# Second MLP product in fp32r: activations and W2 split into high and low parts

## The chip, the cores and the metric

The kernel runs on one core of a Trainium2 chip. The metric is the device time of one execution in microseconds, median of several runs.

## The reference

Layer 0 is a mixture of experts over x of shape (16, 256, 256), 16 units of 256 tokens with 256 features. Layers 1 to 3 are transformer blocks of the same form: modulated layer norm (plain affine in layer 3), self attention with 16 heads of 16, cross attention to 77 context tokens, and an MLP. What the change touches is the MLP of each block, here layer 1's:

```python
x_norm2 = modulate(_ln(x), shift_m, scale_m)
h = jax.nn.gelu(x_norm2 @ W_mlp1 + b_mlp1)
h = h @ W_mlp2 + b_mlp2
x = x + gate_m[:, None] * h
```

W_mlp1 is 256 x 1024, W_mlp2 (called W2 here) 1024 x 256. In layers 2 and 3 the same weights are named fc1_w, fc2_w and ffn_w1, ffn_w2.

## The kernel before, in words

**Two stages.** The function mixture() runs layer 0 for 16 units, one per step. The function blocks() runs layers 1 to 3 as 48 units u (layer u // 16 + 1, input u % 16) in a software pipeline that is written out by hand: every engine (SP, GpSimd, ScalarE, VectorE, TensorE) has its own list of calls, and in the loop over n TensorE does self attention of unit n - 2, cross attention of n - 3, and the MLP of n - 4 and n - 5 in one mixed order. Engines meet through counting semaphores, `S["..."]`. What an engine does next is fixed by its list: a late input holds everything behind it.

**Split products.** Most products of the blocks are done in fp32r with both operands in two parts: high = the value rounded to fp32r, low = value - high. Three products (high by high, low by high, high by low; `TERMS`) are added in PSUM. High parts of activations are made by a cast or copy, low parts by a subtraction. The weights' parts for layers 1 to 3 are made once, in the mixture stage. There a piece of 256 x 256 is loaded into one of two buffers `raw`, ScalarE copies it to the high part (`piece_high`, L920), GpSimd subtracts (`piece_low`, L792), and SP stores both parts to DRAM (`store_piece`, L703). There are 24 pieces, two in each of twelve steps, after the step's other calls. load_piece(k) (L697) waits for piece_low(k - 2), and piece_high(k) also waits for the store of piece k - 2. In blocks() ScalarE's queue loads the parts (`load_split`, L2079) for the next layer once the last unit of a layer has used the old ones.

**The second MLP product** is not split. `up` (L3028, fp32r) makes a quarter of the hidden layer in each of four calls, `up_act` (L1988) applies GELU and writes h_c, and `down(d, j)` (L3183), j from 0 to 7, does two fp32 matmuls each: eight chunks of h_c for the first 128 tokens, then eight for the second. An fp32 matmul shows as two records in the profile. W2 is double buffered between layers, loaded directly with the other weights of `layer_loads`. TensorE does down 0 to 3 in a row and 4 to 7 apart, between the scores of both attentions.

**Around it**, in the same unit of the loop: VectorE takes the row maxima of the self attention's plain scores in eight calls `self_max` (L2477, tile m_a), multiplies the heads by reciprocals (oT_a and oT_b, L2469), and normalises x before cross attention (`cross_normed`, L2439, tile xn_b, not in layer 3); TensorE then turns xn_b (`cross_turned`, L3019) and makes the keys of the next unit from xT_a (L3028), whose two parts VectorE writes (L2519, L2523). GpSimd computes the reciprocal deviations (L1798, L1801), the residual sums (L1790), o_gated (L1848) and the last sum into y_c (L1870). SP copies the head rows q_hl, k_hl, qc_hl into q_cat, k_cat, qc_cat (L1420), 18 DMAs for these three in one unit. In `self_plain` (L3079) TensorE reads q_cat and k_cat.

## Time and profile before

| | us |
|---|---|
| median of 3 runs (2870.46 to 2873.42) | 2873.33 |
| the profiled execution | 2874.42 |
| its span, first to last instruction | 2872.6 |
| TensorE busy (matmuls) | 2745.2, 96% |
| VectorE busy | 1732.0, 60% |
| ScalarE busy | 1548.3, 54% |
| GpSimd busy | 687.1, 24% |

Busy time of an engine is the union of its instructions; matmuls overlap each other, so a length of one matmul is more than its share of a run, and runs are measured from their start to the start of the next instruction. An instruction's row gives its start, its length, and how many alike are merged. The mixture stage fills about the first 650 us, the blocks the rest.

### The profile page before, as it was taken

The page shows a single profiled execution, that of the slowest core. Times are in us where ns is not written, and L with a number is a line of the kernel's source. Part 1 is how long each engine was busy: PE and PEld are TensorE (multiplying, and loading weights), DVE is VectorE, ACT ScalarE, POOL GpSimd, SP SyncE. Part 2 cuts the span into 40 slices and gives each one's busy share as a digit, 9 for nine tenths or more (in the row PEclk, how much of TensorE's full clock was granted, in tenths as well). Part 3 has the DMA queues.
Part 4 walks back from the last instruction along what each step waited for, and adds up shares of the span by engine and source line. Part 5 has one row for each costly group of instructions (what it writes and reads, how often), then busy time and mean ns, then how long its engine had stood idle before and what let it go on. Part 6 is the DMA issues. An engine that isn't in the chain of part 4 may idle for free.

```text
span 2872.6 us, 61852 instructions
## 1 busy us (share of the span) xinstructions
PE 2745.2 (96%) x23508; PEld 2279.8 (79%) x23508; DVE 1732.0 (60%) x3584; ACT 1548.3 (54%) x2703; POOL 687.1 (24%) x759
## 2 busy tenths in 40 slices
PE   7999999995899999999999999999999999999998
PEld 6999999993577777777777777777777777777876
DVE  2444444434676776766766667667566666666642
...
GB/s 162 45 79 80 70 70 70 40 9 132 95 82 116 100 103 122 94 107 124 106 145 97 98 118 93 112 117 93 128 102 136 115 85 112 103 94 105 103 69 38
DMA packets 276950, 277.90 MB, mean 97 GB/s; under 512 B 90352, under 2 KB 206432, under 8 KB 276656
## 3 DMA queue, kind: packets, MB, share of 16 engines
...
## 4 chain that ended last, share of the span: by engine, by line
PE 64%; DVE 7%; issue 3%; ACT 2%; DMA 1%; SPq 0%; POOL 0%; POOLq 0%; DVEq 0%; ACTq 0%
PE gbank L3183 12%; PE obank L3028 10%; PE gbank L3028 7%; PE obank L3035 6%; PE score L3093 4%; PE obank L3113 4%; DVE m_a L2477 4%; PE obank L3159 3%; PE score L3079 3%; PE score L3142 2%; DVE x_a L2439 2%; PE gbank L3128 2%; PE obank L3128 2%; PE gbank L3019 2%; PE gbank L3043 2%
## 5 line engine op out<-in xcount | busy, mean ns | idle before, releaser
L1971 ACT ACTIVATE p_f<-score 128x1024 f32<-128x1024 f32 (+1 forms) x576 | 567.8, 1021 | 293.7 <-PE score L3093 264.6
L2477 DVE TENSOR_REDUCE m_a<-score 128x4 f32<-128x1024 f32 x384 | 459.9, 1219 | 159.0 <-PE score L3079 158.8
L3183 PE MATMUL gbank<-w,h_c 128*128 128x256 f32 x1536 | 387.9, 392 | 1.9 <-ACT h_c L1988 1.9
L3183 PEld LDWEIGHTS gbank<-w,h_c 128*128 128x128 f32 x1536 | 279.2, 191 | 44.9 <-ACT h_c L1988 2.3
L1150 PE MATMUL m_ps<-m_comb,m_w 128*128 128x256 f32 x2304 | 295.4, 284 | 1.5 <-PEq L254 1.5
L1150 PEld LDWEIGHTS m_ps<-m_comb,m_w 128*128 128x128 f32 x2304 | 279.9, 188 | 5.0 <-issue 3.6
L2487 DVE TENSOR_REDUCE m_b<-gbank 128x4 f32<-128x308 f32 x192 | 92.1, 480 | 265.1 <-PE gbank L3128 241.6
L823 ACT ACTIVATE m_hf<-m_ps,tab 128x256 f32<-128x256 f32 x192 | 80.7, 471 | 246.8 <-PE m_ps L1150 246.8
L1848 POOL TENSOR_TENSOR o_gated<-w_o,gate_a 128x512 f32<-128x512 f32 x48 | 62.3, 1298 | 591.0 <-PE obank L3035 591.0
L765 POOL TENSOR_TENSOR m_hhl<-m_hf,m_hhl 128x512 fp32r<-128x512 f32 x96 | 125.3, 1306 | 318.6 <-DVE m_hhl L989 318.6
L3113 PE MATMUL obank<-p_f,v_s 128*20 128x256 f32 x3072 | 199.9, 390 | 0.6 <-ACT p_f L1971 0.4
L3093 PE MATMUL score<-q_cat,k_cat 50*128 50x256 f32 x1536 | 190.2, 318 | 8.4 <-DMA q_cat<-mT_a 6.5
L3093 PEld LDWEIGHTS score<-q_cat,k_cat 50*128 50x128 f32 x1536 | 132.1, 188 | 53.8 <-issue 36.3
L3028 PE MATMUL gbank<-xT_c,w_up 128*128 128x256 f32 x1152 | 170.7, 299 | 2.6 <-DVE xT_c L2519 2.3
L1790 POOL TENSOR_TENSOR res_b<-x_b,b_oc 128x512 f32<-128x512 f32 x48 | 61.2, 1276 | 455.0 <-DVE x_c L2646 455.0
L3028 PE MATMUL obank<-xT_a,w_qkv 128*128 128x256 f32 x1152 | 165.7, 293 | 3.6 <-DVE xT_a L2519 3.2
L989 DVE CAST m_hhl<-m_hf 128x512 fp32r<-128x512 f32 x96 | 41.0, 427 | 212.4 <-ACT m_hf L823 212.4
L3028 PE MATMUL obank<-xT_c,w_up 128*128 128x256 f32 x1152 | 163.3, 292 | 0.1
L3028 PEld LDWEIGHTS gbank<-xT_c,w_up 128*128 128x128 f32 x1152 | 151.2, 196 | 13.1 <-issue 2.7
L3028 PEld LDWEIGHTS obank<-xT_c,w_up 128*128 128x128 f32 x1152 | 145.6, 193 | 19.9 <-issue 19.4
L3079 PE MATMUL score<-k_cat,q_cat 48*128 48x256 f32 x1536 | 155.3, 310 | 5.8 <-DVE m_a L2477 3.6
L3028 PEld LDWEIGHTS obank<-xT_a,w_qkv 128*128 128x128 f32 x1152 | 149.8, 195 | 7.3 <-issue 4.1
...
## 6 DMA issues: line engine op xcount, KB each, us to landing
q_cat<-q_hl SPq DMA_DIRECT2D x288, 128.0 KB, 3.7
k_cat<-k_hl SPq DMA_DIRECT2D x288, 128.0 KB, 4.0
qc_cat<-qc_hl SPq DMA_DIRECT2D x288, 128.0 KB, 3.1
split_L<-m_cut SPq DMA_DIRECT2D x24, 512.0 KB, 5.7
x_a<-x_after_L SPq DMA_DIRECT2D x48, 256.0 KB, 2.7
x_b<-x_after_L SPq DMA_DIRECT2D x48, 256.0 KB, 4.4
kc_cat<-kc_hl SPq DMA_DIRECT2D x288, 39.0 KB, 1.9
x_after_L<-y_c SPq DMA_DIRECT2D x32, 256.0 KB, 2.4
```

What stands on the lines that cost most here:

```text
L765: e.tensor_tensor(h_hl[:, 1, at:at + 2, :], h_f[:, i % 3, :, :], h_hl[:, 0, at:at + 2, :].bitcast(F32), ALU.subtract).then_inc(S["hl"].sem, 1)
L1150: mm = e.matmul(b.ap[:, m, :], w1[:, wp, k, 2 * i + m, :], c[:, cp, k, :], start=(k + wp + cp == 0), stop=(k == 3 and wp == 1))
L1971: e.activation(p_f[i % 4][0:n, :], score[i % 2].ap[0:n, :, :].rearrange("p h n -> p (h n)"), ACT.Exp, scale=SCALE).then_inc(ex.sem, 1)
L2477: e.tensor_reduce(m_a[:, :, i::NPAIR].rearrange("p t h -> p h t"), score[i % 2].ap[:, :, :].rearrange("p h (t k) -> p h t k", t=TT), AX.X, ...
L2487: e.tensor_reduce(m_b[:, :, 8 * hf + 2 * i:8 * hf + 2 * i + 2].rearrange("p t j -> p j t"), B_KP[hf].ap[:, :, :].rearrange("p t (j k) -> p ...
L3028: mm = e.matmul(bank.ap[:, m, :], w[:, wp, i, m * P:(m + 1) * P], xT[:, xp, i, :], start=(wp + xp + i == 0), stop=(xp == 1 and i == CC - 1))
L3035: mm = e.matmul(bank.ap[:, tt, :], xT[:, i, tt * P:(tt + 1) * P], w[:, i, :], start=(i == 0), stop=(i == CC - 1))
L3079: mm = e.matmul(bank.ap[:, hf, tt * NT:(tt + 1) * NT], qm[64 * hf:64 * hf + QROWS, i, tt * P:(tt + 1) * P], km[64 * hf:64 * hf + QROWS, i, ...
L3093: mm = e.matmul(bank.ap[:, hf, kc * NT:(kc + 1) * NT], ka[64 * hf:64 * hf + QROWS + 2, i, kc * P:(kc + 1) * P], qa[64 * hf:64 * hf + QROWS ...
L3113: mm = e.matmul(bank.ap[32 * g:32 * g + VW, i % 2, :], v_s[:, kc, 8 * j + 2 * i + hf, :], pf[:, at:at + NT], start=(kc == 0), stop=(kc == ...
L3128: mm = e.matmul(view[:, j, tt, 0:CPAD], qc_cat[64 * hf:64 * hf + QROWS, 2 * i + j, tt * P:(tt + 1) * P], kc_cat[64 * hf:64 * hf + QROWS, 2 ...
L3183: mm = e.matmul(B_DOWN.ap[:, tt, :], h_c[:, k, tt * P:(tt + 1) * P], weights_of(d)["w2"][:, k, :], start=(k == 0), stop=(k == MC - 1))
```

## The change

`down` becomes a split product: 48 fp32r matmuls a unit in place of 16 fp32 ones. `up_act` writes GELU's result to h_f, two slots of a quarter each. VectorE casts each quarter to h_c's high part (`mlp_h_high`), GpSimd subtracts for the low part (`mlp_h_low`), and `up_act` of quarter i waits for the low part of quarter i - 2. W2 is cut in the mixture stage too: 36 pieces in place of 24, three a step in twelve steps. Its parts are single buffered, 2 MB a layer, loaded by ScalarE's queue after the last unit of a layer has used them (`next_down`).

```diff
         def layer_buffers(stack, i):
             sb = buffers(stack)
             return dict(
-                kvc=sb(f"w_kvc{i}", [P, CC, 2 * D]), w2=sb(f"w_2{i}", [P, MC, D]),
+                kvc=sb(f"w_kvc{i}", [P, CC, 2 * D]),
                 bv=sb(f"b_v{i}", [P, D]), bvc=sb(f"b_vc{i}", [P, D]), boc=sb(f"b_oc{i}", [P, D]))
...
-        split = [None] + [scratch(f"split_L{i}", (8, P, 2 * CC * D)) for i in (1, 2, 3)]
-        W_in = signals(nc, "w", {}, dict(qk=2, v=1, qc=1, up0=2, up1=2, o=1, oc=1))
+        split = [None] + [scratch(f"split_L{i}", (12, P, 2 * CC * D)) for i in (1, 2, 3)]
+        W_in = signals(nc, "w", {}, dict(qk=2, v=1, qc=1, up0=2, up1=2, down=4, o=1, oc=1))
         WT = [None, layer_buffers(root, 1)]
         s_last = nc.alloc_semaphore("last_x_after_L0")
         s_w = [nc.alloc_semaphore(f"weights_L{L}") for L in range(4)]
...
             for i in range(2):
                 loads.append((w["kvc"][:, :, i * D:(i + 1) * D], chunks(kvc[i])))
-            for i in range(0, MC, 2):
-                loads.append((w["w2"][:, i:i + 2, :], chunks(p["w2"][i * P:(i + 2) * P, :])))
             return loads
...
             p = layer_parts(L)
-            return [chunks(w[:, at:at + D]) for w in p["qkv"] + [p["qc"], p["w1"]] for at in range(0, w.shape[1], D)]
-
-        n_w = [0, 9, 9, 9]
+            return ([chunks(w[:, at:at + D]) for w in p["qkv"] + [p["qc"], p["w1"]] for at in range(0, w.shape[1], D)]
+                    + [chunks(p["w2"][at:at + D, :]) for at in range(0, MLP, D)])
+
+        n_w = [0, 5, 5, 5]
...
         N_ITER = NB + 2
+
+        def pieces_of(n):
+            return range(3 * n - 6, 3 * n - 3)
+
...
-                for i in range(2):
-                    store_piece(2 * n - 6 + i)
-                    load_piece(2 * n - 4 + i)
+                for k in pieces_of(n):
+                    store_piece(k - 2)
+                    load_piece(k)
...
-                for i in range(2):
-                    piece_low(2 * n - 4 + i)
+                for k in pieces_of(n):
+                    piece_low(k)
...
-                for i in range(2):
-                    piece_high(2 * n - 4 + i)
+                for k in pieces_of(n):
+                    piece_high(k)
```

In blocks():

```diff
         W = dict(W, qkv=sb("w_qkv", [P, 3, 2, CC, D], F32R), qc=sb("w_qc", [P, 1, 2, CC, D], F32R),
-                 up=sb("w_up", [P, MLP // D, 2, CC, D], F32R))
+                 up=sb("w_up", [P, MLP // D, 2, CC, D], F32R),
+                 down=sb("w_down", [P, MLP // D, 2, CC, D], F32R))
         st_p, st_t, st_k, st_c = stats("p"), stats("t"), stats("k"), stats("c")
         bias_a, gate_a = sb("bias_a", [P, D]), sb("gate_a", [P, D])
...
         bias_c, gate_c = sb("bias_c", [P, D]), sb("gate_c", [P, D])
-        h_c, y_c = sb("h_c", [P, MC, NT]), tile("y_c")
+        h_f, h_c, y_c = sb("h_f", [P, 2, 2, NT]), sb("h_c", [P, 2, MC, NT], F32R), tile("y_c")
 
         score = [Bank(stack.enter_context(nc.psum_tensor(f"score{i}", [P, 2, 512], F32))) for i in range(2)]
...
 
+            def mlp_h_low(c, i):
+                if live(c):
+                    e.wait_ge(*S["C_hh"].at(c, i + 1))
+                    e.tensor_tensor(h_c[:, 1, 2 * i:2 * i + 2, :], h_f[:, i % 2, :, :],
+                                    h_c[:, 0, 2 * i:2 * i + 2, :].bitcast(F32), ALU.subtract).then_inc(S["C_hl"].sem, 1)
+
...
                 e.wait_ge(*S["C_hp"].at(u, i + 1))
-                if u and i == 0:
-                    e.wait_ge(*S["C_down"].at(u - 1))
+                if i >= 2:
+                    e.wait_ge(*S["C_hl"].at(u, i - 1))
+                elif u:
+                    e.wait_ge(*S["C_hl"].at(u - 1, i + 3))
                 for j in range(2):
                     m = 2 * i + j
-                    ac = e.activation(h_c[:, m, :], B_UP[i].ap[:, j, :], gelu,
+                    ac = e.activation(h_f[:, i % 2, j, :], B_UP[i].ap[:, j, :], gelu,
                                       bias=bcols[layer(u)][:, 8 + m:9 + m])
                 ac.then_inc(S["C_h"].sem, 1)
 
...
+            def next_down(d):
+                if last_of_layer(d):
+                    e.wait_ge(*S["C_down"].at(d))
+                    load_split(layer(d) + 1, "down", "down", 8, (0, 1, 2, 3))
+
...
+                load_split(1, "down", "down", 8, (0, 1, 2, 3))
...
                     x_low(c, xn_c[:, :, :], xT_c, S["C_xh"], S["C_xl"])
+
+            def mlp_h_high(c, i):
+                if not live(c):
+                    return
+                e.wait_ge(*S["C_h"].at(c, i + 1))
+                if c and i == 0:
+                    e.wait_ge(*S["C_down"].at(c - 1))
+                e.tensor_copy(h_c[:, 0, 2 * i:2 * i + 2, :], h_f[:, i % 2, :, :]).then_inc(S["C_hh"].sem, 1)
 
             def self_stats(q):
...
             def down(d, j):
                 if not live(d):
                     return
+                tt, i = divmod(j, MC // 2)
                 if j == 0:
-                    e.wait_ge(*S["C_h"].at(d))
+                    weights_in(d, "down")
                     turn(B_DOWN, S["C_y"], d)
-                for i in (2 * j, 2 * j + 1):
-                    tt, k = divmod(i, MC)
-                    mm = e.matmul(B_DOWN.ap[:, tt, :], h_c[:, k, tt * P:(tt + 1) * P], weights_of(d)["w2"][:, k, :],
-                                  start=(k == 0), stop=(k == MC - 1))
+                if tt == 0:
+                    e.wait_ge(*S["C_hh"].at(d, i + 1))
+                for wp, xp in TERMS:
+                    if xp and tt == 0:
+                        e.wait_ge(*S["C_hl"].at(d, i + 1))
+                    for c in range(CC):
+                        mm = e.matmul(B_DOWN.ap[:, tt, :], h_c[:, xp, 2 * i + c, tt * P:(tt + 1) * P],
+                                      W["down"][:, i, wp, c, :], start=(i + wp + xp + c == 0),
+                                      stop=(i == MC // 2 - 1 and xp == 1 and c == CC - 1))
                 if j == MC - 1:
                     mm.then_inc(S["C_down"].sem, 1)
```

The lists of the engines are rotated by some calls in the loop (their bodies start at another place of the same cycle), and the new calls stand in them. Everything else keeps its order on every engine. Where the new calls of VectorE and GpSimd stand, one turn of the loop:

```diff
+                self_max(n - 2, 2)
+                self_max(n - 2, 3)
+                self_max(n - 2, 4)
+                mlp_h_high(n - 5, 0)
+                self_max(n - 2, 5)
+                mlp_h_high(n - 5, 1)
+                self_heads_normed(n - 3)
+                self_max(n - 2, 6)
...
+                cross_stats(n - 3)
+                self_max(n - 2, 7)
+                mlp_h_high(n - 5, 2)
+                cross_normed(n - 3)
+                self_x_high(n - 1)
+                self_x_low(n - 1)
+                self_max_low(n - 2)
+                cross_x_low(n - 3)
                 context_stats(n - 2)
...
+                mlp_h_high(n - 5, 3)
+                cross_heads_normed(n - 4)
```

```diff
+                self_rstd(n - 1)
+                mlp_sum(n - 6)
+                self_residual(n - 3)
+                mlp_h_low(n - 5, 0)
+                mlp_h_low(n - 5, 1)
+                self_out_gated(n - 2)
+                mlp_residual(n - 5)
+                cross_rstd(n - 3)
+                mlp_h_low(n - 5, 2)
+                mlp_h_low(n - 5, 3)
+                cross_residual(n - 3)
```

**VectorE, in a unit of layer 1**, from the statistics of x_b to the parts of xT_b. Before:

```order
L2608 TENSOR_TENSOR vc_s<-obank,b_vc 77x16x16
L2425 BN_STATS t_st<-x_b 128x6 x2
L2430 BN_AGGR t_mv<-t_st 128x2 x2
L2477 TENSOR_REDUCE m_a<-score 128x2x2
L2439 TENSOR_SCALAR xn_b<-x_b,t_mv,t_rstd 128x256 x2
L2519 CAST xT_a<-x_a 128x512
L2523 TENSOR_TENSOR xT_a<-x_a,xT_a 128x512
L2495 TENSOR_TENSOR mT_a<-gbank,mT_a 16x256
L2523 TENSOR_TENSOR xT_b<-gbank,xT_b 128x512
```

Now:

```order
L2735 TENSOR_TENSOR vc_s<-obank,b_vc 77x16x16
L2544 BN_STATS t_st<-x_b 128x6 x2
L2549 BN_AGGR t_mv<-t_st 128x2 x2
L2596 TENSOR_REDUCE m_a<-score 128x2x2
L2670 CAST h_c<-h_f 128x512
L2558 TENSOR_SCALAR xn_b<-x_b,t_mv,t_rstd 128x256 x2
L2638 CAST xT_a<-x_a 128x512
L2642 TENSOR_TENSOR xT_a<-x_a,xT_a 128x512
L2614 TENSOR_TENSOR mT_a<-gbank,mT_a 16x256
L2642 TENSOR_TENSOR xT_b<-gbank,xT_b 128x512
```

A CAST of a quarter of h stands between the last TENSOR_REDUCE of the self scores and xn_b. Two more stand ahead of this place, behind the fifth and the sixth of the eight TENSOR_REDUCE, and one behind xT_b.

**GpSimd, the same unit**, from the sum into x_b to the residual of the next stage. Before:

```order
L1790 TENSOR_TENSOR x_b<-x_b,bias_a 128x512
L1848 TENSOR_TENSOR o_gated<-w_o,gate_a 128x512
L1790 TENSOR_TENSOR res_c<-x_c,bias_c 128x512
L1798 TENSOR_TENSOR t_rstd<-t_mv,eps 128x2
L1801 TENSOR_TENSOR t_rstd<-t_rstd,minus_half 128x2
L1790 TENSOR_TENSOR res_b<-x_b,b_oc 128x512
```

Now:

```order
L1818 TENSOR_TENSOR x_b<-x_b,bias_a 128x512
L1897 TENSOR_TENSOR h_c<-h_f,h_c 128x512 x2
L1876 TENSOR_TENSOR o_gated<-w_o,gate_a 128x512
L1818 TENSOR_TENSOR res_c<-x_c,bias_c 128x512
L1826 TENSOR_TENSOR t_rstd<-t_mv,eps 128x2
L1829 TENSOR_TENSOR t_rstd<-t_rstd,minus_half 128x2
L1897 TENSOR_TENSOR h_c<-h_f,h_c 128x512 x2
L1818 TENSOR_TENSOR res_b<-x_b,b_oc 128x512
```

Two subtractions for h stand ahead of o_gated, and two directly behind t_rstd.

**ScalarE, at the end of a mixture step.** m_cut is the high part of a weight piece, m_hf the next unit's hidden activations. Before:

```order
L904 ACTIVATE m_rex,m_rsm<-m_lg,m_rmx 128x3 x2
L912 ACTIVATE m_gp<-m_gp 128x512
L920 ACTIVATE m_cut<-m_raw 128x512 x2
L823 ACT_TABLE_LOAD
L823 ACTIVATE m_hf<-m_ps,tab 128x256 x2
L843 ACTIVATE m_ctxT<-m_ps 128x154
```

Now:

```order
L907 ACTIVATE m_rex,m_rsm<-m_lg,m_rmx 128x3 x2
L915 ACTIVATE m_gp<-m_gp 128x512
L923 ACTIVATE m_cut<-m_raw 128x512 x3
L826 ACT_TABLE_LOAD
L826 ACTIVATE m_hf<-m_ps,tab 128x256 x2
L846 ACTIVATE m_ctxT<-m_ps 128x154
```

The third copy stands ahead of the table load and the next unit's work.

## Rows read from the trace of the kernel before

**Rows 1.** Busy time by stretch; then granted clock, DMA share, GB/s.

```profile
700.00:2700.00 2000.00, 1937.30 (x17269) 1526.13 (x17270) 1356.48 (x2743) 1184.78 (x1960) 402.02 (x492) 0.99 0.47 108
...
100.00:500.00 400.00, 400.00 (x3251) 391.02 (x3250) 183.13 (x422) 179.24 (x386) 161.95 (x141) 1.00 0.22 74
```

**Rows 2.** Waits of TensorE, 700 to 2700 us: total, times, longest.

```profile
PE gbank L3019 <- ACT h_c L1988: 24.7, 42, 0.6
```

**Rows 3.** Timeline of TensorE, 1500 to 1550 us: start, length, engine, line, tiles.

```profile
1505.37 0.96 PE L3043 MATMUL gbank<-w_qkv,xT_a 128*128 128x256 f32 x6
1506.26 0.46 PE L3142 MATMUL score<-qc_cat,kc_cat 50*77 50x256 f32 x4
...
1524.67 0.60 PE L3019 MATMUL gbank<-ident,xn_b 128*128 128x128 f32 x4
...
1532.37 3.62 PE L3183 MATMUL gbank<-w,h_c 128*128 128x256 f32 x16
1535.91 1.06 PE L3113 MATMUL obank<-p_f,v_s 128*20 128x256 f32 x16
...
1538.05 1.13 PE L3183 MATMUL gbank<-w,h_c 128*128 128x256 f32 x4
1539.11 0.50 PE L3093 MATMUL score<-q_cat,k_cat 50*128 50x256 f32 x4
...
1546.37 0.74 PE L3079 MATMUL score<-k_cat,q_cat 48*128 48x256 f32 x8
...
1549.30 0.96 PE L3043 MATMUL gbank<-w_qkv,xT_a 128*128 128x256 f32 x6
```

**Rows 4.** Timeline of TensorE at the start of a mixture unit.

```profile
360.29 3.05 PE L1150 MATMUL m_ps<-m_comb,m_w 128*128 128x256 f32 x24
363.18 1.01 PE L1215 MATMUL m_ps<-m_ctxT,m_wqk 128*128 128x77 f32 x8
```

**Rows 5.** Timeline of SP's DMA issues, 1528.5 to 1547 us.

```profile
1536.96 4.83 SPq L1420 DMA_DIRECT2D k_cat<-k_hl  x6
```

**Rows 6.** DMA issues: tiles, queue, count, KB each, median us to landing.

```profile
k_cat<-k_hl SPq DMA_DIRECT2D x288, 128.0 KB, 4.0
...
w_up<-split_L ACTq DMA_DIRECT2D x12, 512.0 KB, 5.8
...
m_raw<-in_L_xcond_ffn_w_dram SPq DMA_DIRECT2D x4, 256.0 KB, 4.7
```

**Rows 7.** Timeline of VectorE, 1505 to 1552 us.

```profile
1522.01 1.23 DVE L2477 TENSOR_REDUCE m_a<-score 128x4 f32<-128x1024 f32 x1
1523.76 0.74 DVE L2439 TENSOR_SCALAR xn_b<-x_b,t_mv,t_rstd 128x256 f32<-128x256 f32 x2 [0.52 <-POOL t_rstd L1801]
1524.41 0.42 DVE L2519 CAST xT_a<-x_a 128x512 fp32r<-128x512 f32 x1
1524.86 0.69 DVE L2523 TENSOR_TENSOR xT_a<-x_a,xT_a 128x512 fp32r<-128x512 f32 x1
...
1547.08 1.69 DVE L2439 TENSOR_SCALAR x_a<-x_a,p_mv,p_rstd 128x256 f32<-128x256 f32 x2
```

**Rows 8.** Timeline of GpSimd, 1505 to 1552 us.

```profile
1523.02 0.70 POOL L1801 TENSOR_TENSOR t_rstd<-t_rstd,minus_half 128x2 f32<-128x2 f32 x1
...
1547.24 1.38 POOL L1870 TENSOR_TENSOR y_c<-y_c,res_c 128x512 f32<-128x512 f32 x1 [0.51 <-DVE y_c L2629]
```

**Rows 9.** Timeline of ScalarE at the end of a mixture unit.

```profile
354.41 1.14 ACT L920 ACTIVATE m_cut<-m_raw 128x512 fp32r<-128x512 f32 x2
355.56 1.28 ACT L823 ACT_TABLE_LOAD   x1
359.95 0.84 ACT L823 ACTIVATE m_hf<-m_ps,tab 128x256 f32<-128x256 f32 x2 [3.11 <-PE m_ps L1150]
360.68 0.30 ACT L843 ACTIVATE m_ctxT<-m_ps 128x154 f32<-128x154 f32 x1
```

**Rows 10.** Timeline of GpSimd at the same place.

```profile
355.10 2.52 POOL L792 TENSOR_TENSOR m_cut<-m_raw,m_cut 128x512 fp32r<-128x512 f32 x2 [3.85 <-ACT m_cut L920]
```

More of the change, by code:

```diff
@@ L1900, in _ @@
             self_residual(3)
+            mlp_h_low(1, 0)
+            mlp_h_low(1, 1)
             cross_rstd(3)
             mlp_residual(1)
+            mlp_h_low(1, 2)
+            mlp_h_low(1, 3)
             cross_residual(3)
             self_out_gated(4)
-            for n in range(6, 47):
-                q, a, c, d = n - 1, n - 3, n - 5, n - 6
+            context_rstd(4)
+            mlp_rstd(2)
+            for n in range(7, 47):
+                self_rstd(n - 1)
[9 more added lines that the diff above has]
+                cross_residual(n - 3)
                 if live(n) and n % NB == 0:
@@ L2267, in _ @@
             exp_table(1)
-            for n in range(6, 47):
-                q, m, a, b, c = n - 1, n - 2, n - 3, n - 4, n - 5
+            self_weights(4, 5)
+            self_heads(4, 0)
+            next_rest(6)
+            self_weights(4, 6)
+            self_weights(4, 7)
+            cross_max_high(3)
+            self_heads(4, 1)
+            mlp_modulated(2)
+            cross_weights(3, 0)
+            cross_weights(3, 1)
+            cross_weights(3, 2)
+            cross_heads(3, 0)
+            cross_weights(3, 3)
+            gelu_table(2)
+            context_out(4)
+            cross_heads(3, 1)
+            mlp_act(2, 0)
+            mlp_act(2, 1)
+            cross_keys_high(4)
+            mlp_act(2, 2)
+            for n in range(7, 47):
+                self_modulated(n - 1)
+                self_max_high(n - 2)
+                cross_x_out(n - 3)
+                mlp_act(n - 5, 3)
+                keys_high(n - 1)
+                cross_queries_high(n - 3)
+                exp_table(n - 5)
+                queries_high(n - 1)
+                self_weights(n - 2, 0)
+                self_weights(n - 2, 1)
+                self_weights(n - 2, 2)
+                self_weights(n - 2, 3)
+                self_weights(n - 2, 4)
                 if live(n) and n % NB == 0:
@@ L2825, in _ @@
             self_sum(3)
-            for n in range(6, 47):
-                p, q, m, a, b, c, d = n, n - 1, n - 2, n - 3, n - 4, n - 5, n - 6
+            cross_stats(3)
+            self_max(4, 7)
+            mlp_h_high(1, 2)
+            cross_normed(3)
+            self_x_high(5)
+            self_x_low(5)
+            self_max_low(4)
+            cross_x_low(3)
+            context_stats(4)
+            mlp_h_high(1, 3)
+            cross_heads_normed(2)
+            keys_low(5)
+            cross_queries_low(3)
@@ new lines, in _ @@
+            cross_sum(2)
+            queries_low(5)
+            mlp_stats(2)
+            cross_max(3, 0, 0)
+            cross_max(3, 0, 1)
+            context_normed(4)
+            cross_max(3, 1, 0)
+            cross_max(3, 1, 1)
+            mlp_normed(2)
+            cross_max(3, 2, 0)
+            cross_max(3, 2, 1)
+            cross_max(3, 3, 0)
+            cross_max(3, 3, 1)
+            for n in range(7, 47):
+                self_stats(n - 1)
+                cross_max_low(n - 4)
+                mlp_gated(n - 6)
+                self_normed(n - 1)
+                self_max(n - 2, 0)
+                self_max(n - 2, 1)
+                mlp_x_high(n - 5)
+                mlp_x_low(n - 5)
+                values_out(n - 2)
+                self_recips(n - 3)
+                self_max(n - 2, 2)
[6 more added lines that the diff above has]
+                self_max(n - 2, 6)
+                cross_recips(n - 4)
+                cross_keys_low(n - 3)
+                self_sum(n - 3)
+                cross_values_out(n - 3)
@@ L2878, in _ @@
             cross_x_low(44)
+            mlp_h_high(42, 3)
             keys_low(46)
@@ L3574, in _ @@
                 cross_scores(n - 3, 3)
-                self_plain(n - 1, 2)
-                up(n - 4, 0)
-                self_plain(n - 1, 3)
+            self_plain(45, 2)
+            up(42, 0)
+            self_plain(45, 3)
             self_plain(45, 4)
```

293 lines of the change are left out of this document (183 added, 110 removed).

## The prediction, made before the changed kernel had run

> **What bounds the kernel now.** I first read the busy table by stretch [rows 1]. In the mixture stage TensorE is busy all of 100 to 500 us; in the block stage, 700 to 2700, 1937 of 2000 us, at a granted clock of 0.99, while VectorE has 1356, ScalarE 1185 and GpSimd 402. So TensorE carries the end, and a gap on it costs its full length. The list of waits says how few gaps there are: the largest is 24.7 us in 42 pieces, TensorE waiting for the GELU that frees bank g0 [rows 2]. The other engines stand in a rigid rhythm around TensorE (a unit takes 1549.30 - 1505.37 = 43.9 us [rows 3]), so what decides is whether each thing TensorE needs still comes in time. For that I read one unit of layer 2 on the timelines, engine by engine [rows 3, 5, 7, 8], and the end of one mixture unit [rows 4, 9, 10].
>
> **Part 1, TensorE: the gain.** A unit's second MLP product is now 16 fp32 matmuls, shown as 32 records: one run of 16 and four runs of 4. From start to the next instruction's start the run of 16 takes 1535.91 - 1532.37 = 3.54 us and a run of 4 takes 1539.11 - 1538.05 = 1.06 [rows 3]; I take 1.05 for each of the four, together 7.7 us. The change makes it 48 fp32r matmuls in runs of 24 and four of 6. A run of 24 fp32r matmuls of this shape takes 363.18 - 360.29 = 2.89 us [rows 4]; a run of 6 takes 1506.26 - 1505.37 = 0.89 [rows 3]. New sum 2.89 + 4 x 0.89 = 6.45. Gain: 7.7 - 6.45 = 1.25; since a run of 24 in this stage meets more traffic than in the mixture, I take 1.15 us per unit (bounds 0.9 and 1.25).
>
> **What cuts the gain.** The rows of q_cat and k_cat for the next unit go out by SP in a chain that starts when qc_hl is ready, before this product, and TensorE takes them right after it. SP's last k_cat issue ends at 1536.96 + 4.83 = 1541.79, having begun 0.6 us earlier, and a k_cat transfer lands 4.0 us after its issue: 1545.2. TensorE's self_plain(.,0) starts at 1546.37 [rows 3, 5, 6]. So about 1.1 us of slack faces 1.15 us of gain. Transfers vary, so I count 0.3 us of new DMA wait a unit and keep **0.85 us**.
>
> **Part 2, VectorE and GpSimd: the loss.** Each unit adds four casts (0.42 us, as xT_a's of the same shape [rows 7]) and four GpSimd subtractions (1.26 us each, half of the pair's 2.52 [rows 10], up to 1.38 as y_c's instruction beside VectorE [rows 8]). The first cast comes while VectorE waits for scores anyway: free. The fourth stands ahead of oT_b, where VectorE waits for TensorE: free. The second delays the reductions behind it by 0.4. The third stands straight ahead of xn_b, which TensorE needs for cross_turned. By rows: the last self_max, now 1522.01 to 1523.24 [rows 7], moves to 1522.4 to 1523.6; the third cast ends at 1524.0; xn_b's first half starts there; the cast's end also releases GpSimd's subtraction, whose t_rstd work ends at 1523.72 [rows 8], so it starts at about 1524.1. What then happens the trace shows already: with x_a, GpSimd's y_c starts at 1547.24 during the first half, lasts 1.38, and the two halves of TENSOR_SCALAR, 0.74 for xn_b, take 1.69 and end at 1548.77, 0.15 after GpSimd [rows 7, 8]. The second half waits for the GpSimd instruction. Put on xn_b: 1524.1 + 1.38 + 0.15 = 1525.6 in place of 1524.5. TensorE's cross_turned starts at 1524.67 [rows 3], so it comes 1.0 us late. Behind it xT_a's low part, another 0.42 + 0.69 on VectorE, is late for the fifth matmul of keys by some 0.15. Loss in layers 1 and 2: **1.1 us** a unit. Bounds: 0.3 if GpSimd's start misses the pair (0.4 for the second cast, less the 0.17 us by which xn_b is early), 1.6 if its subtraction gets in ahead of both halves.
>
> The Trainium skill, "SBUF — State Buffer", section "SBUF: two separate sides", says of this port pair that it is "an **exclusive lock**, not a bandwidth split" and that the loser fully blocks for the whole instruction. The rows agree that it waits, but the second half ends 0.15 us after GpSimd's end where a whole half after it would be 0.37 to 0.41. By the rule alone the loss would be 1.35 a unit; the row is what I use.
>
> Layer 3 has no xn_b; there xT_a's cast meets the subtraction. With the third cast at 1523.7 the subtraction runs to 1525.1, the cast ends near 1525.25 in place of 1524.83, and its low part adds 0.15: **0.6 us** (bounds 0.1 and 0.9). ScalarE's new waits (h_f has two slots) cost nothing: GELU 2 waits for the first subtraction, and between the two lie TensorE's work for cross_keys_values, self_projected and a whole up().
>
> **Part 3, the mixture: three pieces a step.** Per step ScalarE gets one more copy of 0.57, GpSimd 1.28, SP one store and one load. The work fits; the order does not. There are two raw buffers, so the third load waits until GpSimd has finished the step's first piece, 355.10 + 1.26 = 356.4; SP issues store and load by 356.9; an m_raw load lands 4.7 us after issue [rows 6, 10], with two stores and two loads in flight; here there is one of each, and I take 4.2: 361.1. ScalarE stands at that copy. Behind it are the table load (1.28), the next unit's first hidden activation (0.84) and m_ctxT (0.30), which ended at 360.98 [rows 9]: 361.1 + 0.6 + 1.28 + 0.84 + 0.30 = 364.1. TensorE wants m_ctxT at 363.18 [rows 4]. So **1.0 us** on TensorE, twelve times: **+12 us**. Bounds: nothing, if the load lands 1 us sooner, and 2.6 a step with the 5.8 us of a w_up load [rows 6], so 0 to +31; I am near the 4.7 row, which is the same transfer.
>
> **Part 4, the rest.** At two layer changes ScalarE issues four more 512 KB loads between GELU 0 and GELU 1, so GELU 1, its cast and oT_a come late; a w_up load of that size lands in 5.8 us [rows 6] and W2's are wanted some 16 us later, so they arrive. I count 1.5 us each, +3. The first units get the same four loads early, and casts while TensorE still waits: +2. At the end the last product is short by itself: -2.
>
> **Sum.** Units 2 to 31: 30 x (1.1 - 0.85) = +7.5. Layer 3: 16 x (0.6 - 0.85) = -4. Mixture +12, layer changes +3, start +2, end -2. Together +18.5. The profiled execution took 2874.42 us (span 2872.6), 1.1 over the median of 2873.33; against its own time the sum gives 2892.9, against the median about **2892 us**.
>
> **Rivals.**
> A, faster: the third subtraction does not hit xn_b, or only its tail. For it: the race is decided within 0.1 us, there is a gap of 0.52 us before xn_b already [rows 7], and TensorE keeps 0.85 a unit. Then units 2 to 47 give 46 x (0.3 - 0.85) = -25, with mixture 6 and the rest +3: 2857; with the full 1.15 kept, 2843. It decides from a loss below 0.85 a unit. Against it: x_a's pair has just this spacing.
> B, slower still: the mixture's third load lands as late as 5.8 us. TensorE loses 2.6 a step: +31 in place of +12, 2911. Against it: no second store behind this load.
> C, the two sides cancel: loss 0.85, mixture about 5: 2873 to 2879.
> D, the fp32r matmuls do not run at the price of rows 3 and 4 in this place, so there is no gain: 46 x 0.85 = +39, 2931.
> E, the second half of xn_b runs in full after GpSimd: 30 x 0.25 = +7.5, 2900. The Trainium skill's page "SBUF — State Buffer" would have it so.
>
> **Chances.** Forecast (2885 to 2900) 0.32, A 0.30, B 0.12, C 0.16, D 0.03, E 0.07. A difference of 0.2% (5.7 us) is about what a measurement of this kernel can tell. C splits: 0.12 within it, 0.04 slower; A gives 0.30 faster. Faster 0.30, same 0.12, slower 0.58. The range leaves out D and the far ends of A and B: **2848 to 2918**. As both signs hold much of the chance, the forecast's own range is 2885 to 2900.
>
> **What would show it.** Right: TensorE waits for xn_b about 1 us in each unit of layers 1 and 2; xn_b's pair grows from 0.74 to about 1.7; unit period 44.1 to 44.3 in layers 1 and 2 and about 43.7 in layer 3; runs of 24 and 6 at 3.0 and 0.88; TensorE waits for q_cat or k_cat rows before self_plain; in the mixture a gap of about 1 us before the m_ctxT matmuls, in twelve of the sixteen units. Wrong: no xn_b wait and a period near 43 would give A; a gap near 2.6 us there gives B; down runs that are no shorter give D.

## The result, and the profile after

| | before | changed |
|---|---|---|
| median | 2873.22 (6 runs, 2866.67 to 2878.26) | 2889.47 (6 runs, 2886.60 to 2894.52) |
| ratio to before | | 1.0061, 95% interval 1.0046 to 1.0076 |
| the profiled execution, its span | 2874.42, 2872.6 | 2888.95, 2887.1 |
| TensorE busy | 2745.2 | 2716.0 |
| VectorE, GpSimd busy | 1732.0, 687.1 | 1834.0, 949.1 |

The change makes the kernel 0.6% slower, 16 us; the forecast was 2892 us. TensorE is busy for 29 us less and still ends 14.5 us later. By stretch, as in [rows 1] (busy time of each engine, then granted clock, DMA share, GB/s):

```profile
700.00:2700.00 2000.00, 1895.60 (x17771) 1526.04 (x17771) 1438.72 (x2899) 1176.58 (x1952) 618.88 (x658) 0.98 0.46 110
100.00:500.00 400.00, 398.29 (x3225) 388.20 (x3224) 181.74 (x421) 185.90 (x396) 174.50 (x151) 1.00 0.28 92
```

TensorE was busy 1937 of 2000 us in the blocks and is now busy 1896: it has gaps that it had not. The list of its waits for 700 to 2700 us (total, times, longest), as in [rows 2]:

```profile
PE gbank L3225 <- ACT h_f L2068: 24.7, 42, 0.6
PE gbank L3225 <- DVE xn_b L2558: 23.3, 30, 2.7
PE score L3285 <- issue: 18.6, 25, 2.6
PE score L3348 <- DVE m_a L2596: 9.7, 24, 0.9
```

The first line is as before. The second is new: xn_b, in nearly every unit of layers 1 and 2. The fourth was 19.3 us in 43 waits before. No term of the sum had this fall of about 10 us; it is there in the later kernels too, and its cause was not looked for. The third is self_plain; where the profile says "issue", the semaphore waited for is that of the rows of k_cat, whose last transfer lands 0.09 us earlier. One unit of layer 1 on TensorE's timeline, as in [rows 3]:

```profile
1232.28 0.38 PE L3262 MATMUL gbank<-ident,m_a 128*16 128x128 f32 x2
1233.32 0.66 PE L3225 MATMUL gbank<-ident,xn_b 128*128 128x128 f32 x4 [0.66 <-DVE xn_b L2558]
...
1240.94 3.18 PE L3394 MATMUL gbank<-w_down,h_c 128*128 128x256 f32 x24
1244.04 1.06 PE L3319 MATMUL obank<-p_f,v_s 128*20 128x256 f32 x16
1246.18 0.96 PE L3394 MATMUL gbank<-w_down,h_c 128*128 128x256 f32 x6
...
1254.21 0.74 PE L3285 MATMUL score<-k_cat,q_cat 48*128 48x256 f32 x8 [0.29 <-issue]
```

From m_a to xn_b it takes 1.04 us where it took 0.21, from this row of the kernel before to xn_b's at 1524.67 in [rows 3]:

```profile
1524.46 0.38 PE L3056 MATMUL gbank<-ident,m_a 128*16 128x128 f32 x2
```

The reason stands on VectorE's and GpSimd's timelines, which answer to [rows 7, 8]:

```profile
1229.85 1.21 DVE L2596 TENSOR_REDUCE m_a<-score 128x4 f32<-128x1024 f32 x1
1230.97 0.42 DVE L2670 CAST h_c<-h_f 128x512 fp32r<-128x512 f32 x1
1231.57 1.69 DVE L2558 TENSOR_SCALAR xn_b<-x_b,t_mv,t_rstd 128x256 f32<-128x256 f32 x2 [0.18 <-POOL t_rstd L1829]
```

```profile
1230.84 0.70 POOL L1829 TENSOR_TENSOR t_rstd<-t_rstd,minus_half 128x2 f32<-128x2 f32 x1
1231.50 1.29 POOL L1897 TENSOR_TENSOR h_c<-h_f,h_c 128x512 fp32r<-128x512 f32 x1
```

The end of t_rstd frees both sides at once: xn_b may start, and so may the subtraction behind t_rstd in GpSimd's list, since the cast that it needs has long ended. The subtraction comes first by 0.07 us and xn_b's pair takes 1.69 instead of 0.74, in every unit from 4 to 31.

**Where the 14.5 us come from.** I compared the starts of the instruction that writes v_s, one per unit, in the two profiled executions:

| stretch | the prediction's terms | after minus before |
|---|---|---|
| up to unit 0 (mixture) | +12 | 675.8 - 673.1 = +2.7 |
| units 0 to 5 (start) | +2 | 232.9 - 216.5 = +16.4 |
| units 5 to 36 (layers 1 and 2, both changes) | +7.5, +3 | 1376.4 - 1372.9 = +3.5 |
| units 36 to 47 (layer 3) | -4 | 476.9 - 480.5 = -3.6 |
| behind it | -2 | 125.1 - 129.6 = -4.5 |
| sum | +18.5 | +14.5 |

The total came out well by luck: the mixture was priced 9 us too high and the units 5 to 36 by 7, and against that the start 14 too low. In layers 1 and 2 the usual unit (what most units take from one v_s to the next) has not grown at all: the median is 43.9 us before and after, so the collision eats the gain and no more. And these are two single executions. In the five further kernels with the same loads at the start, units 0 to 5 took 224.2 to 230.4 us, so part of the 16.4 is this execution's own.

**The start.** ScalarE now issues 2 MB of W2's parts at 700.77 us behind the 2.5 MB of the other weights. TensorE, and windows of 10 us (after, then before):

```profile
714.93 1.06 PE L3319 MATMUL obank<-p_f,v_s 128*20 128x256 f32 x16
718.64 0.80 PE L3285 MATMUL score<-k_cat,q_cat 48*128 48x256 f32 x4 [2.65 <-DMA q_cat<-q_hl]
...
719.82 1.92 PE L3319 MATMUL obank<-p_f,v_s 128*20 128x256 f32 x16
```

```profile
710.00:720.00 10.00, 7.35 (x74) 3.49 (x68) 0.52 (x1) 5.00 (x7) 0.00 (x0) 0.67 0.75 201
720.00:730.00 10.00, 9.10 (x49) 5.97 (x42) 5.85 (x8) 1.36 (x4) 0.00 (x0) 0.50 0.12 26
730.00:740.00 10.00, 8.47 (x34) 6.79 (x34) 6.31 (x11) 0.00 (x0) 0.00 (x0) 0.50 0.18 47
```

```profile
710.00:720.00 10.00, 8.85 (x88) 5.82 (x88) 7.41 (x11) 3.78 (x8) 0.00 (x0) 1.00 0.10 24
720.00:730.00 10.00, 7.24 (x50) 6.03 (x48) 9.32 (x19) 1.52 (x4) 0.89 (x2) 1.00 0.25 68
```

The rows of unit 1 land late, while the weights are loaded, and TensorE stands for 2.65 us. The last two transfers of q_cat, issued from 707.55 on (view of 708 to 716 us), take 10.2 us to land, where the median for q_cat in these first units was 3.1:

```profile
q_cat<-q_hl SPq DMA_DIRECT2D x2, 128.0 KB, 10.2
```

What follows costs more than the gap: the clock, which had just risen (16 matmuls in 1.06 us), falls back, the same 16 take 1.92 us, and for 720 to 740 us the granted clock is 0.50, the lower of the two levels, where before it was 1.00 from 710 to 730. From unit 0's values to unit 1's it takes 65.5 instead of 53.8 us. The other 4.7 us of the start lie in units 1 to 5, 3.2 of them between units 4 and 5.

**The mixture.** ScalarE, then SP, then TensorE at the place of [rows 4, 9]:

```profile
361.54 0.63 ACT L923 ACTIVATE m_cut<-m_raw 128x512 fp32r<-128x512 f32 x1 [4.45 <-DMA m_raw<-in_L_xcond_fc_w_dram]
...
364.21 0.30 ACT L846 ACTIVATE m_ctxT<-m_ps 128x154 f32<-128x154 f32 x1
```

```profile
358.34 0.43 SPq L700 DMA_DIRECT2D m_raw<-in_L_xcond_fc_w_dram  x1
```

```profile
364.72 1.01 PE L1218 MATMUL m_ps<-m_ctxT,m_wqk 128*128 128x77 f32 x8
```

The chain is as predicted step by step, but the load lands at 361.5, 3.2 us after its issue, not 4.2. m_ctxT ends at 364.51, 0.21 us before it is wanted. Only in two of the twelve steps, where the load took 3.7 and 4.1 us, does TensorE wait (1.5 us in all).

### The profile page after: what moved, and what is told of

It reads as the page before. It is cut to its first block, busy times and chain, and to the rows that moved or that the text cites. A ratio compares the mean times of both kernels' runs of the same rounds, so it can differ in the third digit from the quotient of the medians.

```text
span 2887.1 us, 64022 instructions
## 1 busy us (share of the span) xinstructions
PE 2716.0 (94%) x24276; PEld 2292.3 (79%) x24276; DVE 1834.0 (64%) x3776; ACT 1554.4 (54%) x2715; POOL 949.1 (33%) x963
## 4 chain that ended last, share of the span: by engine, by line
PE 58%; DVE 6%; issue 5%; POOL 2%; DMA 2%; SPq 2%; ACT 1%; ACTq 0%; POOLq 0%; DVEq 0%
PE gbank L3394 9%; PE obank L3234 8%; PE obank L3241 6%; PE gbank L3234 6%; PE obank L3319 5%; PE score L3299 4%; PE obank L3365 3%; PE score L3285 3%; DVE m_a L2596 2%; PE score L3348 2%; PE gbank L3249 2%; PE gbank L3334 2%; PE obank L3334 2%; PE gbank L3225 2%; PE obank L3468 1%
## 5 line engine op out<-in xcount | busy, mean ns | idle before, releaser
L1897 POOL TENSOR_TENSOR h_c<-h_f,h_c 128x512 fp32r<-128x512 f32 x192 | 246.4, 1284 | 640.5 <-DVE h_c L2670 640.5
L3394 PE MATMUL gbank<-w_down,h_c 128*128 128x256 f32 x2304 | 336.5, 294 | 1.2 <-POOL h_c L1897 1.2
L3394 PEld LDWEIGHTS gbank<-w_down,h_c 128*128 128x128 f32 x2304 | 292.4, 190 | 16.0 <-POOL h_c L1897 1.6
L768 POOL TENSOR_TENSOR m_hhl<-m_hf,m_hhl 128x512 fp32r<-128x512 f32 x96 | 125.1, 1303 | 267.2 <-DVE m_hhl L992 267.2
L3285 PE MATMUL score<-k_cat,q_cat 48*128 48x256 f32 x1536 | 159.0, 315 | 28.7 <-issue 18.6
L3234 PE MATMUL obank<-xT_a,w_qkv 128*128 128x256 f32 x1152 | 172.9, 297 | 5.5 <-DVE xT_a L2638 3.4
L3285 PEld LDWEIGHTS score<-k_cat,q_cat 48*128 48x128 f32 x1536 | 111.6, 192 | 64.8 <-issue 30.1
```

What stands on the lines that cost most here:

```text
L768: e.tensor_tensor(h_hl[:, 1, at:at + 2, :], h_f[:, i % 3, :, :], h_hl[:, 0, at:at + 2, :].bitcast(F32), ALU.subtract).then_inc(S["hl"].sem, 1)
L1897: e.tensor_tensor(h_c[:, 1, 2 * i:2 * i + 2, :], h_f[:, i % 2, :, :], h_c[:, 0, 2 * i:2 * i + 2, :].bitcast(F32), ALU.subtract).then_inc(S ...
L3234: mm = e.matmul(bank.ap[:, m, :], w[:, wp, i, m * P:(m + 1) * P], xT[:, xp, i, :], start=(wp + xp + i == 0), stop=(xp == 1 and i == CC - 1))
L3285: mm = e.matmul(bank.ap[:, hf, tt * NT:(tt + 1) * NT], qm[64 * hf:64 * hf + QROWS, i, tt * P:(tt + 1) * P], km[64 * hf:64 * hf + QROWS, i, ...
L3394: mm = e.matmul(B_DOWN.ap[:, tt, :], h_c[:, xp, 2 * i + c, tt * P:(tt + 1) * P], W["down"][:, i, wp, c, :], start=(i + wp + xp + c == 0), ...
```

## Experiments

All edits are made on the changed kernel, if nothing else is said. Times are medians with the ratio to the kernel before, run beside it (its median was 2871.3 to 2874.0 us each time). The intervals are 4 to 6 us wide to either side, so differences of a few microseconds rest on the traces alone.

**h2_later.** The collision taken away by order alone.

```diff
                 self_max(n - 2, 7)
-                mlp_h_high(n - 5, 2)
                 cross_normed(n - 3)
                 self_x_high(n - 1)
                 self_x_low(n - 1)
+                mlp_h_high(n - 5, 2)
```

> Edit: in the loop, VectorE's cast of the third quarter of h stands behind xT_a's low part instead of ahead of xn_b, so that GpSimd's subtraction can't start with xn_b. Theory (the subtraction beside xn_b's pair costs TensorE 0.66 us in each of 28 units): xn_b's pair 0.74 instead of 1.69 us, no wait of TensorE for xn_b, period of layers 1 and 2 about 43.2, total 18 us under the changed kernel: 2871, ratio to before 0.999. Rival (the rows of q_cat and k_cat end the unit anyway): the wait before self_plain grows from 0.29 by as much, total stays near 2889. Second rival (the subtraction now falls on xT_b's low part or the queries and stretches them): half of it comes back, 2880.

Measured: 2859.7 us (8 runs), ratio 0.9957 [0.9939, 0.9974]: 30 us under the changed kernel, and faster than before. VectorE and GpSimd at the same place (this execution, 2868.68 us, was the slowest of the eight):

```profile
1225.37 0.74 DVE L2558 TENSOR_SCALAR xn_b<-x_b,t_mv,t_rstd 128x256 f32<-128x256 f32 x2 [0.53 <-POOL t_rstd L1829]
1226.03 0.42 DVE L2638 CAST xT_a<-x_a 128x512 fp32r<-128x512 f32 x1
```

```profile
1227.59 1.30 POOL L1897 TENSOR_TENSOR h_c<-h_f,h_c 128x512 fp32r<-128x512 f32 x1 [2.25 <-DVE h_c L2670]
```

The pair is 0.74 again and TensorE's wait for xn_b is gone; the usual unit takes 42.8 us (median in layers 1 and 2 43.0, where the changed kernel has 43.9). The expectation missed layer 3, where I had said that nothing moves. There the same cast met xT_a's; in the changed kernel, and then with the edit:

```profile
2473.82 0.94 DVE L2638 CAST xT_a<-x_a 128x512 fp32r<-128x512 f32 x1 [0.71 <-ACT x_a L2030]
```

```profile
2458.12 0.43 DVE L2638 CAST xT_a<-x_a 128x512 fp32r<-128x512 f32 x1 [1.04 <-ACT x_a L2030]
```

Its usual unit goes from 43.2 to 42.7 us. Both rivals fall, since the total is 11 us below even the theory's; the waits before self_plain do grow, but only from 18.6 to 23.2 us in 850 to 2700. The 28 waits of 0.66 and eleven units of 0.5 in layer 3 make 24 of the 30 us; the other 6 I could not place. Between the two profiled executions, of which this one is slow for its kernel, units 5 to 36 differ by 10.9 us and layer 3 by 2.4, with longer single waits for rows here (up to 3.3 us) and a mean granted clock of 0.970 instead of 0.974. Units 2 and 3, which wait 1.25 and 1.46 us for xn_b in the changed kernel, keep their old order here.

**low2_waits.** The cast stays ahead of xn_b, and only GpSimd moves.

```diff
                 cross_rstd(n - 3)
+                if live(n - 3) and layer(n - 3) < 3:
+                    e.wait_ge(*S["T_xn"].at(n - 3))
                 mlp_h_low(n - 5, 2)
```

> Edit: the cast stays ahead of xn_b, but GpSimd waits for xn_b's end before it subtracts. Theory (the overlap with GpSimd is the cost, not the cast): xn_b's pair is 0.74, TensorE doesn't wait for xn_b, and the collision moves to xT_a's cast right behind, which grows from 0.41 to between 1.0 and 1.5 us; TensorE waits 0.3 to 1.0 us for xT_a; total 2880 to 2895. Rival (the cast of 0.42 us ahead of xn_b is the cost, GpSimd is innocent): TensorE's wait for xn_b stays at 0.66 in each unit, xn_b's pair stays 1.69 or starts later by as much, total 2889.

Measured: 2893.11 us, ratio 1.0070 [1.0055, 1.0084]. VectorE, GpSimd, TensorE, and TensorE's largest wait from 700 to 2700 us:

```profile
1234.11 0.73 DVE L2560 TENSOR_SCALAR xn_b<-x_b,t_mv,t_rstd 128x256 f32<-128x256 f32 x2 [0.19 <-POOL t_rstd L1829]
1234.76 0.42 DVE L2640 CAST xT_a<-x_a 128x512 fp32r<-128x512 f32 x1
1235.21 1.66 DVE L2644 TENSOR_TENSOR xT_a<-x_a,xT_a 128x512 fp32r<-128x512 f32 x1
```

```profile
1234.92 1.39 POOL L1897 TENSOR_TENSOR h_c<-h_f,h_c 128x512 fp32r<-128x512 f32 x1 [0.85 <-DVE xn_b L2560]
```

```profile
1236.92 1.22 PE L3236 MATMUL obank<-xT_a,w_qkv 128*128 128x256 f32 x8 [0.83 <-DVE xT_a L2644]
```

```profile
PE obank L3236 <- DVE xT_a L2644: 24.9, 30, 0.9
```

With the cast in place and GpSimd out of the way, xn_b takes 0.73 and isn't waited for: the cast is innocent, the overlap is the cost. It moved on to the next instruction that it could hold. I had named xT_a's cast; that one came in first and made GpSimd wait (1.39 instead of 1.27 to 1.30), and it was the low part, a TENSOR_TENSOR with both inputs in SBUF, that grew from 0.69 to 1.66.

The Trainium skill, "SBUF — State Buffer", section "SBUF: two separate sides", names as what meets GpSimd on the shared ports operations in a two-port mode or with two SBUF inputs, and says that whichever starts first has the pair. The trace doesn't name modes, but the instructions that waited are of the kinds that the page lists, and in both kernels the one that came first went on. It says too that the other fully blocks. They do stand until GpSimd's end, but what is left of a blocked instruction then is less than its length alone: xT_a's low part ends 0.56 us after it (0.69 alone), layer 3's cast 0.28 after (0.42 alone), the first half of xn_b's pair 0.15 after (0.40 alone). Only the second half of the pair runs in full, 0.40, so that the pair ends 0.47 after GpSimd. Minimum, median and longest of the 64 halves in the changed kernel, in ns, with the blocked ones the longest:

```profile
L2558 DVE TENSOR_SCALAR xn_b<-x_b,t_mv,t_rstd x64: 392/402/1378, 743.0 to 2123.1; 128x256 f32<-128x256 f32 x64
```

So what rival E of the prediction said, the second half in full behind GpSimd, did happen, but it cost nothing more than forecast, because GpSimd started ahead of the pair and not within it.

**no_parts.** The gain without what it costs. With the parts go GELU's waits for the slots of h_f.

```diff
-                    ac = e.activation(h_f[:, i % 2, j, :], B_UP[i].ap[:, j, :], gelu,
+                    ac = e.activation(h_c[:, 0, m, :], B_UP[i].ap[:, j, :], gelu,
...
-                        mm = e.matmul(B_DOWN.ap[:, tt, :], h_c[:, xp, 2 * i + c, tt * P:(tt + 1) * P],
+                        mm = e.matmul(B_DOWN.ap[:, tt, :], h_c[:, 0, 2 * i + c, tt * P:(tt + 1) * P],
```

> Leaves out: the casts and the subtractions of h (GELU writes the high part itself, and the low part's product reads the high part). All 48 fp32r matmuls, all loads and the mixture stage stay. Theory (the loss in layers 1 and 2 is the one collision, all other casts and subtractions are covered): period of layers 1 and 2 about 43.2 as in layer 3, which doesn't move; total 2889 - 18 - 3 = about 2867. Rival (the casts on VectorE cost elsewhere too, in layer 3 as well): layer 3's period falls below 43.0 and the total below 2857.

Measured: 2846.71 us, ratio 0.9918 [0.9899, 0.9936]. The usual unit takes 42.7 us in layers 1 and 2 and in layer 3. So the rival's numbers came out: layer 3 does move. But its reason, casts that cost elsewhere too, holds for little: in h2_later all casts and subtractions stay, and its usual units are only 0.1 us longer than these. Of the 13 us between the two medians that makes 5; another 4 lie in units 0 to 5 (224.2 against 227.8 us), and the rest is not placed.

**ramp_later.**

```diff
             def first_of_the_rest():
...
-                load_split(1, "down", "down", 8, (0, 1, 2, 3))
...
             self_weights(2, 7)
+            load_split(1, "down", "down", 8, (0, 1, 2, 3))
             self_heads(2, 1)
```

> Edit: the four first loads of W2's parts (2 MB) stand in ScalarE's queue behind the last exponentials of unit 2 (at about 810 us) instead of at 700 us. Theory (the burst delays the rows of unit 1, TensorE stands 2.65 us at self_plain and drops to the lower clock for some 15 us): the interval from unit 0's to unit 1's values goes back from 65.5 to about 54 us, total 2878, ratio to before 1.0017. Rival (the start is slower through the casts and subtractions or by where the clock happened to rise): interval stays near 65, total 2887 to 2890.

Measured: 2883.13 us, ratio 1.0035 [1.0022, 1.0048], 6 us under the changed kernel's. Windows, to be read against those above:

```profile
710.00:720.00 10.00, 9.06 (x94) 4.51 (x86) 2.35 (x2) 5.96 (x8) 0.00 (x0) 0.73 0.25 56
720.00:730.00 10.00, 8.11 (x51) 6.10 (x52) 9.87 (x16) 0.54 (x2) 0.00 (x0) 0.95 0.16 34
```

The 2.65 us gap is gone and the clock stays up; the interval is 56.5 us. The theory holds, its size was half right: in five other kernels with the burst in its old place the interval was 61.1 to 62.6 us, so 65.5 was a high reading, and the burst is worth about 6 us, not 11. The interval stays 2.7 us over the 53.8 of the kernel before.

**next_down_early.** The loads at the two layer changes. In the changed kernel gate_a's rows, issued at 1534.64 us just behind them, landed only at 1541.55, 6.9 us later, and TensorE stood 2.70 us for xn_b.

```diff
                 cross_weights(n - 3, 0)
+                next_down(n - 5)
                 cross_weights(n - 3, 1)
...
                 mlp_act(n - 4, 0)
-                next_down(n - 5)
                 mlp_act(n - 4, 1)
```

> Edit: at the two layer changes ScalarE issues the four loads of W2's parts behind the first cross exponential (about 7 us sooner, in a stretch in which the DMA engines are nearly idle). Theory (the burst at 1533.5 us holds back gate_a's rows, landing at 1541.55, so o_gated, t_rstd and xn_b come late and TensorE stands 2.70 us): that wait shrinks to the usual 0.66, the same at the second change; total 4 us less, 2885. Rival (other transfers, the rows of q_cat and k_cat, are held back instead): no change within 2 us, 2889.

Measured: 2889.24 us, ratio 1.0070 [1.0051, 1.0089]: no gain. Its wait for xn_b around the first change, and its longest around the second:

```profile
PE gbank L3225 <- DVE xn_b L2558: 0.6, 1, 0.6
```

```profile
PE score L3285 <- issue: 4.5, 2, 4.2
```

The long wait at the first change did go (3.4 us in two waits became 0.6); ramp_later and no_w2_cut, with the loads in the old place, have it too, 2.5 us each (h2_later and low2_waits, where the collision is moved, wait 0.8 and 1.0). At the second change TensorE stood 4.2 us before self_plain. That can't be laid to the moved loads: with the loads where they were the same wait was 2.0 to 4.0 us in the six kernels that have them there (2.6 in the changed one). The kernel before has none there over 1.5 us, so the second change has a cost of its own that this edit doesn't touch.

**no_w2_cut.** Pieces of W2 dropped from the list, two a step.

```diff
         def pieces_of(n):
-            return range(3 * n - 6, 3 * n - 3)
+            return range(2 * n - 4, 2 * n - 2)
```

> Leaves out: the cutting of W2 into parts in the mixture stage (two pieces a step as before); the blocks load the parts of the first MLP weight in its place, same bytes, same places. Theory (the third piece's load lands 3.2 us after its issue and ScalarE is free just in time in ten of twelve steps): the mixture stage gets 3 us shorter, its steps 37.1 to 37.5 us again, total 2886. Rival (the prediction's term, 1.0 us in each of twelve steps): 12 us shorter, 2877.

Measured: 2887.69 us, ratio 1.0049 [1.0030, 1.0068]. The steps are 37.1 to 37.5 us as before, and unit 0 is reached at 673.9 instead of 675.8. The mixture's share is 2 to 3 us by the traces. The median alone could not tell that from nothing, but it does refute the prediction's 12: 2877 would be a ratio of 1.0015, outside the interval.

**best.** h2_later (in units 0 and 1 of the written-out start too), ramp_later and next_down_early together.

```diff
+            self_x_low(4)
+            mlp_h_high(0, 2)
...
+            self_x_low(5)
+            mlp_h_high(1, 2)
```

> Edit: the third cast behind xT_a's low part (in the prologue's two units as well), the first loads of W2's parts behind unit 2's exponentials, and the loads at the layer changes ahead. Theory (the three costs lie at different places and add): 2859.7 from the first edit, less 6 for the start, 4 for the layer changes and 2 for the prologue's two units: about 2848, ratio to before 0.992. Rival (the rows of q_cat and k_cat, already the last to land in most units, take up what is won): 2855 to 2860.

Measured: **2854.34 us**, ratio 0.9942 [0.9927, 0.9957], 19 us under the kernel before and 35 under the changed one. Its interval overlaps that of h2_later, so nothing shows that the two edits more than that one gained anything. The waits for xn_b in units 2 and 3, 1.25 and 1.46 us, are down to one of 0.25; from unit 4 to unit 5 it takes 42.4 us, but this interval was anything from 43.7 to 46.3 in the kernels with the old order. The total is 6 us over my sum and nearly what the rival said, while TensorE's waits before self_plain are 20.4 us in 850 to 2700, no more than in the other kernels (18.6 to 25.2).

**rows_by_act** and **high_rows_by_act**, both on best: the transfers of k_cat issued by ScalarE, all six or the four of the high part.

```diff
-                key_rows_high(n - 1)
-                key_rows_low(n - 1)
+                if n < 7:
+                    key_rows_high(n - 1)
+                    key_rows_low(n - 1)
                 load_residual(n - 2)
...
                 self_weights(n - 2, 1)
+                key_rows_by_act(n - 1, 0)
+                key_rows_by_act(n - 1, 1)
                 self_weights(n - 2, 2)
```

(The new function holds SP's waits and DMAs of the same rows, for units 6 to 43. The second kernel moves part 0 alone and leaves key_rows_low with SP.)

> Edit on top of the version with all three moves: the six k_cat transfers of a unit are issued by ScalarE, behind its second exponential, where it waits 3.6 us for scores, instead of by SP behind the twelve of qc_cat and q_cat. Theory (the rows of q_cat and k_cat are what TensorE now waits for before self_plain: mean of the piece from the first fp32r run's end to self_plain is 10.25 to 10.49 us where 9.80 is free of waits, besides single waits of 1 to 2.4 us): the rows land 2 to 3 us sooner, the piece is 9.8, total 15 to 30 us less, 2825 to 2840. Rival (ScalarE's six issues of 0.5 us make the fourth exponential late and TensorE waits for p_f instead): total 2850 to 2870.

> Edit: the same with only the four k_cat transfers of the high part issued by ScalarE. Theory (rows are the bound, ScalarE's room is 3.6 us): rows land about 2 us sooner, total as with all six or up to 5 us better, 2825 to 2840. Rival (ScalarE's issues cost): less of it, 2845 to 2860.

Measured: 3147.22 us, ratio 1.0959 [1.0937, 1.0980], and 3149.71 us, ratio 1.0950 [1.0927, 1.0973]. Neither theory had this. In the second kernel, the issues with their time to landing, one unit of TensorE, TensorE's largest wait from 950 to 2600 us, and two windows:

```profile
qc_cat<-qc_hl SPq DMA_DIRECT2D x6, 128.0 KB, 4.0
q_cat<-q_hl SPq DMA_DIRECT2D x6, 128.0 KB, 8.1
k_cat<-k_hl ACTq DMA_DIRECT2D x4, 128.0 KB, 5.6
```

```profile
1239.38 0.30 PE L3348 MATMUL gbank<-kc_cat,qc_cat 48*128 48x78 f32 x1 [2.02 <-DMA qc_cat<-qc_hl]
...
1243.74 1.91 PE L3333 MATMUL obank<-p_f,v_s 128*20 128x256 f32 x16
```

```profile
PE gbank L3348 <- DMA qc_cat<-qc_hl: 81.1, 32, 4.0
```

```profile
950.00:2600.00 1650.00, 1536.84 (x12906) 1244.63 (x12898) 1025.85 (x2116) 853.83 (x1412) 459.68 (x492) 0.87 0.47 96
1238.00:1252.00 14.00, 12.62 (x83) 10.18 (x84) 5.39 (x15) 5.80 (x7) 0.03 (x1) 0.57 0.68 109
```

In the changed kernel the issues of q_cat and k_cat, all on SP's queue, land after a median of

```profile
q_cat<-q_hl SPq DMA_DIRECT2D x6, 128.0 KB, 3.4
k_cat<-k_hl SPq DMA_DIRECT2D x6, 128.0 KB, 4.0
```

Two things follow. The 18 transfers of a unit are not held by the one queue alone: in one queue, with issues 0.64 us apart, they land 0.78 us apart on average (the first at 1240.85, the last at 1254.12), and from two they land no denser (0.86, from 1232.42 to 1247.08). In windows of 16 us around them the DMA engines were busy for 0.80 of the time with one queue and 0.99 with two, and moved about the same, 164 and 160 GB/s; what holds the rows in the one queue is not shown. The second queue let k_cat's rows in among those of qc_cat, which are wanted first. And a gap of 2.0 us in front of the first of the small cross attention products (kc_cat by qc_cat), once per unit, costs 8 (in the mean of 32 units the gap is 2.5 us): the granted clock is 0.57 in the 14 us from there on, 16 matmuls take 1.91 again, and the usual unit takes 51 us. That the gap brings the clock down is read from their order; no run sets it apart.

## Why the prediction came out

By its own steps, each with what it measured:

- **TensorE's gain, 1.15 a unit.** The run of 24 takes 3.11 us (3.55 before), the runs of 6 0.89 each (medians of 40 and 160 runs, start to the next start). One thing was not in the sum: the product starts 0.19 us sooner behind oT_b's (5.51 instead of 5.70 us from the start of the cross queries), and in units without a wait the stretch from the end of down's first run to self_plain, with the four runs of 6 in it, takes 9.80 us instead of 10.45. Gain 0.44 + 0.19 + 0.65 = 1.28, borne out by no_parts, whose usual unit is 1.2 us under the 43.9 before. Right, and slightly too low; rival D is out.
- **DMA wait, 0.3 a unit.** That same stretch has medians of 9.9 to 10.3 us by layer where 9.80 is free of waits, and means of 10.1 to 10.5: 0.1 to 0.5, or 0.3 to 0.7 in the mean. Right in kind and size. The slack was rightly read off [rows 3, 5, 6]; SP's chain is not bound by its one queue alone, as high_rows_by_act shows.
- **xn_b's pair 1.7, TensorE 1.0 late, keys 0.15 more.** Pair 1.69; 0.82 late; 0.11 more: 0.93 in place of 1.1. One detail was wrong: GpSimd starts 0.07 us ahead of the pair, not in its first half. It makes no difference to its length. Cause shown by h2_later and low2_waits. Rival A needed GpSimd's start to miss the pair; it hits it every time, since one semaphore frees both.
- **Units of layers 1 and 2.** The forecast was 44.1 to 44.3 us, 0.25 more than before. Measured were 44.03 in the mean over units 5 to 15 and 44.29 over 17 to 31, where it was 44.02 and 44.07; the medians are 43.9 before and after. So the collision and the gain, each sized within 0.2 us, cancel, and the +7.5 of the sum is not there in the usual unit.
- **Layer 3, xT_a's cast meeting the subtraction, 0.6 a unit.** The cast grew by 0.52 us; h2_later takes 0.5 off the unit. Usual unit 43.2, below the forecast 43.7; all of layer 3 gained 3.6 us, with 4 forecast.
- **The mixture, +12.** The step that failed: "here there is one of each, and I take 4.2". It is 3.2, which is the bound that the prediction gave for no cost at all: TensorE waits for m_ctxT in two steps and not in twelve. Rival B is out.
- **The start, +2.** The second step that failed. The same four loads were priced at the layer changes and found early enough for their own use; what they keep back was not asked. They delay small transfers that TensorE waits for, and the clock falls behind the wait. Of the 16.4 us about 6 are these loads' (ramp_later); the rest is in part this execution's own and in part not placed.
- **Layer changes +3.** The 31 units between 5 and 36 lose 3.5 us where 7.5 and 3 were forecast, 2.0 of it the 2.70 us wait behind gate_a. Single units differ by up to 3 us between the two executions for other reasons (one right behind a gap with a low clock in the kernel before took 49.4 us), so this term isn't measured more closely.
- **The total.** 2892 against 2889.5 is luck: the terms miss by 14, 9 and 7 us, and the misses cancel. What came out by its mechanism is the unit: gain, collision and rows.
